# A gated cross-attention layer on one core: the context products of four heads made, rounded and subtracted in one go

## What is computed

```python
q_hk = (layernorm(x) @ Wq.T).reshape(B, S, 16, 128)
q_big = rope(einsum('bshk,hkq->bshq', q_hk, w_kc_q))          # 192 wide
kv_r = rope(ctx)                                              # 64 wide
q_r = einsum('bshq,hqr->bhsr', q_big, W_qr)
k_r = einsum('bld,hdr->bhlr', kv_r, W_kr)
attn = softmax(einsum('bhsr,bhlr->bhsl', q_r, k_r))
ctx_c = einsum('bhsl,bld->bhsd', attn, kv_r)                  # the context product
x = x + tanh(g0) * (einsum('bhsd,hkd->bhsk', ctx_c, w_kc_kv) merged over heads) @ Wo.T
x = x + tanh(g1) * experts(layernorm(x))                      # top 8 of 64
```

## Time and profile before

| | us |
|---|---|
| median of 3 executions | 306.44 (304.74 to 307.68) |
| the profiled execution's own time | 306.0 |
| its span, first to last instruction | 306.0 |
| TensorE busy | 286.0 (93%) |
| VectorE busy | 195.0 (64%) |
| ScalarE busy | 150.6 (49%) |
| GpSimd busy | 135.4 (44%) |

### The profile page before, as it was taken

How to read it: one execution, slowest core, us unless ns; L and a number is a source line. 1 busy time by engine, 2 the same in 40 slices (tenths; PEclk the granted TensorE clock), 3 DMA queues, 4 the chain that set the end, 5 groups by cost and what they waited for, 6 DMA issues and landing times.

```text
span 306.0 us, 5002 instructions
## 1 busy us (share of the span) xinstructions
PE 286.0 (93%) x1672; PEld 207.7 (68%) x1672; DVE 195.0 (64%) x454; ACT 150.6 (49%) x451; POOL 135.4 (44%) x210
## 2 busy tenths in 40 slices
PE   7899799999998999999998999999989997899786
PEld 7883587487746786678657784778467844768463
DVE  3686896377726765567547862777368735677664
ACT  1402655475238363664456363852473627656332
POOL 2856068325732555037613743257416742333103
PEclk9999999999999999999999999999999997999975
DMA  8972030035000000450000000000000000001012
GB/s 227 384 205 77 1 87 2 1 126 159 2 0 0 2 2 0 122 163 2 0 0 2 1 0 2 0 0 3 0 2 2 0 2 0 0 2 34 2 36 69
DMA packets 13787, 13.17 MB, mean 43 GB/s; under 512 B 4226, under 2 KB 13122, under 8 KB 13634
## 3 DMA queue, kind: packets, MB, share of 16 engines
q1 hardware_dynamic: 13234, 12.46, 13.3%
q10 hardware_dynamic: 528, 0.39, 0.4%
HBM read 11.80 MB, written 1.05 MB: 42 GB/s over the span
## 4 chain that ended last, share of the span: by engine, by line
PE 75%; DVE 13%; issue 4%; ACT 3%; POOL 3%; DMA 1%; ACTq 0%; DVEq 0%; POOLq 0%
PE ring L884 21%; PE context L1005 9%; PE ring L894 8%; PE probs_t L993 7%; PE scores L982 6%; DVE q_stack L651 6%; PE ring L922 6%; PE ring L905 5%; PE scores L983 4%; PE ring L959 2%; PE ring L854 2%; ACT q_stack L572 2%; PE ring L945 1%; PE ring L862 1%; DMA x_sb<-in_x 1%
## 5 line engine op out<-in xcount | busy, mean ns | idle before, releaser
L481 POOL TENSOR_SCALAR probs<-probs,inv_sum 128x256 f32<-128x256 f32 x128 | 59.9, 483 | 108.5 <-DVE inv_sum L800 108.5
L447 POOL TENSOR_TENSOR roped<-roped,cross 128x512 f32<-128x512 f32 x48 | 60.7, 1286 | 29.6 <-DVE cross L665 29.5
L581 ACT ACTIVATE probs<-scores,neg_max 128x256 f32<-128x256 f32 x128 | 60.0, 479 | 12.2 <-DVE neg_max L794 11.9
L591 ACT COPY probs_t_sb<-probs_t 128x512 f32<-128x512 f32 x64 | 37.8, 591 | 52.6 <-PE probs_t L993 52.5
L794 DVE TENSOR_REDUCE neg_max<-scores 128x2 f32<-128x512 f32 x64 | 43.4, 679 | 7.0 <-PE scores L983 7.0
L982 PE MATMUL scores<-keys_hi,q_stack 128*128 128x256 f32 x128 | 40.1, 335 | 7.4 <-DVE q_stack L651 4.9
L651 DVE TENSOR_TENSOR q_stack<-ring,q_stack 64x512 fp32r<-64x512 f32 x32 | 22.0, 688 | 30.8 <-ACT q_stack L572 30.3
L664 DVE TENSOR_TENSOR roped<-ring,rope_q_sb 128x512 f32<-128x512 f32 x48 | 33.0, 688 | 11.9 <-PE ring L884 11.0
L982 PEld LDWEIGHTS scores<-keys_hi,q_stack 128*128 128x128 f32 x128 | 24.3, 190 | 23.5 <-issue 14.2
L884 PE MATMUL ring<-xn_hi,a_hi 128*128 128x512 f32 x96 | 39.1, 407 | 0.9 <-DVE a_lo L651 0.6
L993 PE MATMUL probs_t<-ident,probs 128*128 128x128 f32 x256 | 39.0, 275 | 0.8 <-POOL probs L481 0.5
(11 more groups left out here) (90 smaller groups left out, 447.0 us busy)
## 6 DMA issues: line engine op xcount, KB each, us to landing
wq_sb<-in_wq SPq DMA_DIRECT2D x4, 512.0 KB, 4.7
wo_t_sb<-in_wo_t SPq DMA_DIRECT2D x4, 512.0 KB, 4.9
w_qr_sb<-in_w_qr SPq DMA_DIRECT2D x4, 384.0 KB, 3.3
rope_q_sb<-in_rope_q SPq DMA_DIRECT2D x1, 1536.0 KB, 8.8
w_kc_q_sb<-in_w_kc_q SPq DMA_DIRECT2D x3, 384.0 KB, 4.6
x_sb<-in_x SPq DMA_DIRECT2D x4, 256.0 KB, 6.8
w_kr_sb<-in_w_kr SPq DMA_DIRECT2D x4, 192.0 KB, 3.7
out<-x_sb SPq DMA_DIRECT2D x3, 256.0 KB, 2.2
```

The costliest lines, as they stand in the source:

```text
L447: last = nc.gpsimd.tensor_tensor(roped[:, j, k, :], roped[:, j, k, :], cross[:, done % 2, j, :], ALU.add)
L481: last = nc.gpsimd.tensor_scalar(e, e, inv_sum[:, i % 4, half:half + 1], 1.0, ALU.mult, ALU.mult)
L581: last = nc.scalar.activation(probs[:, i % E_BUFS, half, :], scores[:, i % 2, half, :], ACT.Exp, bias=neg_max[:, i % 4, half:half + 1], ac ...
L591: nc.scalar.copy(probs_t_sb[:, i % T_BUFS], probs_t[:]).then_inc(probs_t_ready, 1)
```

## The change

Two context groups are made in one slot: the four heads of a batch. A new function, `contexts_at(i)`, says which groups slot i makes, and all three engines use it. Groups 2k and 2k + 1 are made in slot 5 of a step (items 0 to 3) and slot 1 of the next (items 4 to 7); slots 3 and 7 make none. The last four groups stay apart, in slots 3, 5 and 7 of step 7 and behind the loop. The second group of a double one writes the other 256 columns of the bank, ScalarE copies 128x512 at once and VectorE subtracts 128x512 at once; in the last groups each takes the half of its pair. As items wait longer for their product, `probs_t_sb` gets eight buffers in place of four; `xn` lies over the first four as before. The number of matmuls doesn't change. 14 of the 32 copies and 14 of the 32 subtractions go.

```diff
--- before.py
+++ after.py
@@ -31,7 +31,7 @@
 STEPS = GROUPS * TOKENS // SPAN
 ITEMS = GH * 2
 RING = 4
-E_BUFS, T_BUFS = 4, 4
+E_BUFS, T_BUFS = 4, 8
 SHARED_FROM = 4
 WARM_UP = 40
 LEAD = 2
@@ -254,7 +254,7 @@
         cross = sb("cross", [P, 2, 2, SPAN])
         probs = sb("probs", [P, E_BUFS, 2, L])
         probs_t_sb = sb("probs_t_sb", [P, T_BUFS, 2, S])
-        xn = probs_t_sb[:, :, :, :].rearrange("p a b d -> p (a b) d")
+        xn = probs_t_sb[:, 0:CHUNKS // 2, :, :].rearrange("p a b d -> p (a b) d")
 
 
         xn2 = roped[:, :, :, :].rearrange("p a b c -> p (a b c)")[:, 0:TOKENS * D // P].rearrange(
@@ -337,6 +337,19 @@
             n, s = divmod(i, ITEMS)
             b, pair = s // 4, s // 2 % 2
             return n, 2 * pair + s % 2, b
+
+        def context_of(qs, into):
+
+            n, head, b = item_of(2 * qs[0])
+            pair, w = head // 2, len(qs)
+            at = into[:, n % 2, pair:pair + w, b * S:(b + 1) * S]
+            return at, context[:, pair * S:(pair + w) * S].rearrange("p (a s) -> p a s", a=w)
+
+        def contexts_at(i):
+
+            if i >= items - ITEMS + 3:
+                return [i // 2 - 1] if i % 2 else []
+            return [(i - 5) // 2, (i - 5) // 2 + 1] if i >= 5 and i % 4 == 1 else []
 
         def last_item(n, pair=None, batch=None):
 
@@ -590,12 +603,13 @@
                     act.wait_ge(context_ready, (i - T_BUFS) // 2 + 1)
                 nc.scalar.copy(probs_t_sb[:, i % T_BUFS], probs_t[:]).then_inc(probs_t_ready, 1)
 
-            def copy_context(q):
-
-                n, head, b = item_of(2 * q)
-                act.wait_ge(context_ready, q + 1)
-                nc.scalar.copy(context_hi[:, n % 2, head // 2, b * S:(b + 1) * S],
-                               context[:, 0:S]).then_inc(context_hi_ready, 1)
+            def copy_contexts(qs):
+
+                w = len(qs)
+                if not w:
+                    return
+                act.wait_ge(context_ready, qs[-1] + 1)
+                nc.scalar.copy(*context_of(qs, context_hi)).then_inc(context_hi_ready, w)
 
 
             act.wait_ge(filled, 4)
@@ -607,14 +621,13 @@
             for n in range(STEPS):
                 for s in range(ITEMS):
                     i = n * ITEMS + s
-                    if i >= 3 and i % 2 == 1:
-                        copy_context(i // 2 - 1)
+                    copy_contexts(contexts_at(i))
                     pieces(steps[n][s][0])
                     copy_transposed(i)
                     if i + LEAD < items:
                         exponentials(i + LEAD)
                     pieces(steps[n][s][1])
-            copy_context(items // 2 - 1)
+            copy_contexts([items // 2 - 1])
             pieces(after)
 
 
@@ -675,13 +688,15 @@
                     dve.wait_ge(ring_free, freed[u])
                     variances(c, w, stats2_ready, moments2_ready, var2_ready)
 
-            def context_low(q):
-
-                n, head, b = item_of(2 * q)
-                at = (slice(None), n % 2, head // 2, slice(b * S, (b + 1) * S))
-                dve.wait_ge(context_hi_ready, q + 1)
-                nc.vector.tensor_tensor(context_lo[at], context[:, 0:S], context_hi[at].bitcast(F32), ALU.subtract
-                                        ).then_inc(context_lo_ready, 1)
+            def contexts_low(qs):
+
+                w = len(qs)
+                if not w:
+                    return
+                dve.wait_ge(context_hi_ready, qs[-1] + 1)
+                dst, src = context_of(qs, context_lo)
+                nc.vector.tensor_tensor(dst, src, context_of(qs, context_hi)[0].bitcast(F32), ALU.subtract
+                                        ).then_inc(context_lo_ready, w)
 
             def maxima2(u, c, w):
 
@@ -811,13 +826,12 @@
                         inverse(i + 1)
                     if i + LEAD < items and s != 6:
                         maxima(i + LEAD)
-                    if i >= 3 and i % 2 == 1:
-                        context_low(i // 2 - 1)
+                    contexts_low(contexts_at(i))
                     pieces(steps[n][s][0])
                     if i + LEAD < items and s == 6:
                         maxima(i + LEAD)
                     pieces(steps[n][s][1])
-            context_low(items // 2 - 1)
+            contexts_low([items // 2 - 1])
             pieces(after)
 
 
@@ -994,15 +1008,21 @@
                                                    probs[:, i % E_BUFS, half, kc * P:(kc + 1) * P], ident[:])
                 last.then_inc(transposed, 1)
 
+            def make_contexts(qs):
+
+                if qs and qs[0]:
+                    pe.wait_ge(context_lo_ready, qs[0])
+                for q in qs:
+                    make_context(q)
+
             def make_context(q):
 
                 n, head, b = item_of(2 * q)
+                at = slice(head // 2 * S, (head // 2 + 1) * S)
                 pe.wait_ge(probs_t_ready, 2 * q + 2)
-                if q:
-                    pe.wait_ge(context_lo_ready, q)
                 for kc in range(2):
                     for e in range(2):
-                        last = nc.tensor.matmul(context[64 * e:64 * e + 64, 0:S],
+                        last = nc.tensor.matmul(context[64 * e:64 * e + 64, at],
                                                 keys[:, ((n % 2) * 2 + b) * 2 + kc, 0, :],
                                                 probs_t_sb[:, (2 * q + e) % T_BUFS, kc, :],
                                                 start=(kc == 0), stop=(kc == 1))
@@ -1019,8 +1039,7 @@
             for n in range(STEPS):
                 for s in range(ITEMS):
                     i = n * ITEMS + s
-                    if i >= 3 and i % 2 == 1:
-                        make_context(i // 2 - 1)
+                    make_contexts(contexts_at(i))
                     if i + LEAD < items and s != 6:
                         make_scores(i + LEAD)
                     pieces(steps[n][s][0])
@@ -1028,7 +1047,7 @@
                         make_scores(i + LEAD)
                     turn_probs(i)
                     pieces(steps[n][s][1])
-            make_context(items // 2 - 1)
+            make_contexts([items // 2 - 1])
 
             pieces(after)
 
```

## The result

The changed kernel takes 313.45 us (median of 4 runs, 313.26 to 316.45), the kernel before took 307.06 us in the same session (304.74 to 307.94). The ratio is 1.026, with an interval from 1.019 to 1.032: slower by 2.6% (the medians alone give 2.1%), where 2.2% was forecast, and the time is 0.35 us from the one forecast.

A forecast was written before the change was run, and what follows sets the result against it. TensorE's in-order queue (93% busy, 75% of the chain) was taken to set the pace. Second groups cost 11.7 us, emptied slots return 5.0; 6.7 on the median 306.44 gives 313.1 us, range 310 to 316.

The forecast's parts named there:

- Slot 7 gives nothing back: Slot 7 of steps 1 to 5: turns already wait for GpSimd's scaling, so removing the group gains 0 us.
- the unshown places: Slot 3 of step 6, slot 7 of steps 0 and 6: taken as 0.4 us given back each, 1.2 in all.
- Slots 3: Removing slot 3's group gives back 0.65 us in steps like 3, 0.73 like 2, 0.35 in step 0.
- The second group costs 0.9 us: In slots 5 and 1, a group behind another adds 0.9 us; 13 of the 14 places count, 11.7 us.
- The last one, in step 7: The second group in slot 1 of step 7 costs nothing, hidden in TensorE's 0.84 us wait for VectorE.
- The sum: 11.7 us taken by second groups less 5.0 given back by emptied slots: 6.7 us slower.
- ScalarE and VectorE at nothing: Merged copies (2.3 us saved) and subtractions (at most 5.8) are hidden behind other waits and count as 0.
- How the forecast stood to the median: The profiled execution before, taken as 306.0 us, was put 0.4 under the median of three runs, 306.44.
- The third rival: More idle time at five step ends lowers TensorE's clock: 5 us, 318; chance 0.15, shared with a dearer second group.
- What would show it: Profile after: 16-matmul groups of 1.9 to 2.0 us, slot 7 turns waiting about 1, TensorE waits +12, busy -4.

The follow-up runs named there:

- The filler in slot 7: Changed kernel plus one repeated, unread context group at the start of slot 7 in steps 0 to 6, 56 matmuls more: 313.23 us, ratio 1.019.

## Why the prediction was right, point by point

- **Slot 7 gives nothing back.** Right for steps 1 to 5: the shift across it falls by 0.06 us in the odd steps and by 0.01 in the even ones, and the 0.06 is lost again by the next turn (+0.05 in step 4). The turn at 134.55 waits 1.16 us where about 1 was said. The filler in slot 7 shows it as free time. In the unshown places the 0.4 was a poor guess, either way: slot 7 gave 0.33 us in step 0 and 0.78 in step 6, and slot 3 of step 6 gave 0.18. That their sum is 1.3 against 1.2 is luck.
- **Slots 3.** Forecast 0.65 in the odd steps, 0.73 in the even ones, 0.35 in step 0. Measured 0.72 (4.29 to 3.57 in step 3), 0.69 (3.23 to 2.54 in step 2) and 0.32. All given back comes to 3 x 0.72 + 2 x 0.69 + 0.32 + 1.3 = 5.2 against 5.0.
- **The second group costs 0.9 us.** The rows have 1.95 - 1.08 = 0.87, the shift grows by 0.87 in slot 1 and by 0.86 to 0.92, 0.89 in the mean, in slot 5. 7 x 0.89 + 6 x 0.87 is 11.5 us for 13 of them, where 11.7 was forecast. The last one, in step 7, was to vanish in a wait of 0.84 us; 0.60 of its 0.86 us did.
- **The sum.** 11.5 + 0.26 - 5.2 = 6.6 us from these terms, 6.6 in the shift of the last turn, 6.7 forecast. Two errors of 0.2 to 0.3 us, the cheaper second group and the rest of the last one, cancel in what is taken; what is given back came out 0.2 larger.
- **ScalarE and VectorE at nothing.** Right, by the kernel with single copies. Only the sizes of the savings were off. The groups by form:

```profile
L698 DVE TENSOR_TENSOR context_lo<-context,context_hi 128x512 fp32r<-128x512 f32 x14 | 9.5, 680 | 0.0
...
L612 ACT CAST context_hi<-context 128x512 fp32r<-128x512 f32 x14 | 8.2, 586 | 16.7 <-PE context L1025 16.7
```

  One subtraction of 680 ns stands for two of 415, which saves 150 ns, not up to 415; the copy saves 168 ns. VectorE's busy time fell by 1.7 us and ScalarE's by 0.5, less than the 2 to 5 that was said. The Trainium skill's "VectorE: DVE Perf Modes", section on the errata of SBUF-source operations, has the direction right (the source here is PSUM in part), and none of it reaches the path.
- **How the forecast stood to the median.** Here a step was wrong. I took the span of 306.0 for the execution's own time. Every run here has its time 1.75 to 1.93 us above its span (316.45 against 314.6, 304.73 against 302.9), so the profiled execution of before took near 307.8, which is 1.4 over the median and not 0.4 under it. The forecast came out at median plus 6.7 all the same; built on the execution's own time it would have been 314.5, 1.1 us over the measured median.
- **TensorE's clock.** The third rival was true in part. The windows of the changed kernel (us, then busy time of PE, PEld, DVE, ACT and POOL, granted clock, DMA share, GB/s):

```profile
99.00:104.00 5.00, 4.68 (x18) 3.91 (x19) 2.56 (x6) 2.21 (x9) 1.86 (x4) 0.66 0.00 0
236.00:240.00 4.00, 4.00 (x14) 3.14 (x13) 1.99 (x5) 1.02 (x4) 1.57 (x4) 0.57 0.01 2
266.00:271.00 5.00, 4.79 (x29) 4.58 (x27) 2.93 (x6) 2.30 (x10) 1.87 (x4) 0.66 0.00 0
```

  The first two stand behind the ends of steps 1 and 5, where a group had been removed; in the trace of before only the third has a counterpart. A granted clock of 0.66 is mostly the lower of the two levels (1.2 and 2.4 GHz). The jumps of the shift price each at 1.44 and 1.67 us. But the kernel with the same TensorE queue and single copies, profiled at 313.31 us, has neither, and three of the changed kernel's four runs lie at 313.3 to 313.6. So the price isn't paid at five step ends; it was paid at two of them in the one execution that has it on record, and what decides this stays open.
- **What would show it.** The 16-matmul groups at 1.95 us and the turns' waits came as said. Two signs were off. TensorE's listed waits grew by some 8 us, not 12. At 134.55 the list shows 1.16 us idle for a gap of 1.43 between starts: the removed time lies partly under the modelled ends of the matmuls in front. And TensorE's busy time rose from 286.0 to 287.5 us instead of falling by 4, because matmuls at the lower clock take longer. With single copies and without these two stretches it is 283.2, a fall of 2.8.

## What to carry to other kernels

In a kernel that one in-order queue bounds, a piece of work is worth its place, not its length: taken from a slot where the queue waits for another engine next, it gives nothing, and put ahead of a long chain it costs its whole length. So look for the slots with a hole behind them and move work into these, and check at each what reads the moved result, since a reader that stays right behind its producer pays the whole latency of the engines between. Read an effect of a few us against an execution's clock stretches, position by position, before it is put down to the edit.

## What the runs showed of the hardware that was not expected

- **Times come in steps.** The times of the kernel before gather near 304.5, 306.1, 307.7 and 309 us. In the traces one stretch at the lower clock more or less goes with one step: 1.44 and 1.67 us in the changed kernel's shift. The end of the run is at the lower clock in every trace, and where that begins differs too: at 294.1 us in the trace of before, at 295.8 in that of the kernel with eight buffers, which took 304.73 us. Why a stretch falls where it does was not settled. One began right behind an idle time of 0.78 us that elsewhere had no effect, in the changed kernel's timeline:

```profile
99.32 0.36 PE L996 MATMUL scores<-keys_hi,q_stack 128*128 128x256 f32 x1 [0.78 <-ACT probs L594]
...
100.07 0.63 PE L898 MATMUL ring<-xn_hi,a_hi 128*128 128x512 f32 x1
100.50 0.63 PE L898 MATMUL ring<-xn_lo,a_hi 128*128 128x512 f32 x1
```

  Those start 0.43 us apart, and 0.23 at the end of step 3 (168.75 and 168.98). The Trainium skill's "TensorE: Matmul & The Clock Gate", Part 1, says that the throttled state is the default and that activity lifts it. The rows agree in direction; they don't say which idle time is one too many.
- **More matmuls, no more time.** With 56 filler matmuls in slot 7 the queue is 1.1 us longer, and the median is that of the changed kernel (313.23 and 313.45 us). Its trace has only one stretch at lower clock ahead of the end, where that of the changed kernel has three. Four runs don't settle that fillers prevent such stretches.
- **A boundary between groups costs nothing.** Within the double group at 155.23 the pairs of matmuls start 0.22 us apart, over the boundary too (155.93 and 156.15), and the second group costs four such spacings. A lone group is worth 0.3 us more, and the rows of before place that at its two ends: the group at 160.74 starts 0.20 us after the last matmul of the turn, where scores without a group start 0.03 us after it, and the scores start 0.32 us after the group's last pair. That the cause is the change of shape was not tested apart.
